# Two-layer transformer on one core: the last expert run writes its output tiles to their tokens' places, with new orders of work

## The reference

```
h = layernorm(x) * (1 + ca) + sa ;  x = x + ga * attention(h)
h = layernorm(x) * (1 + cb) + sb ;  x = x + gb * experts(h)
```

```
for e in range(16):
    h = silu(xf @ W1[e] + b1[e]) * (xf @ W11[e] + b11[e])
    y = y + (h @ W2[e] + b2[e]) * gates[:, e, None]      # gates: 0 for all but the best two
z = silu(xf @ Ws1 + bs1) * (xf @ Ws11 + bs11) @ Ws2 + bs2
```

## Time and profile before

| | us |
|---|---|
| median of three runs | 1138.53 (1136.83 to 1141.62) |
| the profiled execution's own time | 1138.8 |
| its span, first to last instruction | 1137.1 |
| PE busy | 893.5 (79%) |
| DVE busy | 803.9 (71%) |
| ACT busy | 550.6 (48%) |
| POOL busy | 436.4 (38%) |
| mean granted clock of TensorE | 0.887 |

### The profile page before, as it was taken

The page is one execution under the profiler, slowest core; times in us unless marked ns, Lnnn a source line. Parts: engine busy times, 40 slices in busy tenths (PEclk is TensorE's granted clock), DMA queues, the critical chain, the costliest instruction groups (busy, mean ns, idle before and its releaser), DMA issues.

```text
span 1137.1 us, 17345 instructions
## 1 busy us (share of the span) xinstructions
PE 893.5 (79%) x5709; PEld 560.6 (49%) x5709; DVE 803.9 (71%) x1942; ACT 550.6 (48%) x1353; POOL 436.4 (38%) x623
## 2 busy tenths in 40 slices
PE   7743076896798799779878898987989998997892
PEld 5422033454345447555333554444656665665692
DVE  4688988958998843357667766668667778846664
ACT  3635244345344324316544454534667755685372
POOL 0213253462393413203345224444542427834422
PEclk9866597898798899989988898879999988999797
DMA  7500000000100000232222102214347625362473
GB/s 215 173 0 1 1 0 1 1 0 1 32 1 1 1 1 1 85 102 91 68 74 94 66 1 65 85 46 160 124 126 228 193 76 161 107 202 69 146 239 108
DMA packets 69416, 89.49 MB, mean 79 GB/s; under 512 B 7072, under 2 KB 41520, under 8 KB 69296
## 3 DMA queue, kind: packets, MB, share of 16 engines
q1 hardware_dynamic: 67280, 84.20, 23.8%
q0 software_dynamic: 2048, 4.20, 1.2%
HBM read 62.56 MB, written 26.35 MB: 78 GB/s over the span
## 4 chain that ended last, share of the span: by engine, by line
PE 33%; DVE 11%; ACT 6%; issue 4%; POOL 3%; DMA 2%; SPq 0%; POOLq 0%; ACTq 0%; DVEq 0%
PE banks L870 8%; PE banks L1030 6%; DVE MX L1543 3%; PE banks L963 3%; PE banks L1004 3%; PE banks L901 2%; ACT PT L1861 2%; PE banks L970 2%; POOL oms L2046 2%; ACT yh L1795 1%; PE banks L912 1%; DVE sil L1493 1%; PE banks L1017 1%; PE banks L945 1%; ACT sil L1801 1%
## 5 line engine op out<-in xcount | busy, mean ns | idle before, releaser
L1543 DVE TENSOR_REDUCE MX<-banks 128x4 f32<-128x512 f32 (+2 forms) x192 | 199.2, 1043 | 74.1 <-PE banks L1004 73.2
L1861 ACT ACTIVATE PT<-banks 128x768 f32<-128x768 f32 (+1 forms) x192 | 167.6, 879 | 111.7 <-PE banks L963 111.1
L2023 POOL TENSOR_SCALAR_AFFINE_SELECT PT<-PT 128x256 f32<-128x256 f32 x256 | 107.2, 434 | 200.7 <-ACT PT L1861 200.4
L970 PE MATMUL banks<-KS,QS 32*128 32x512 f32 (+3 forms) x512 | 95.4, 418 | 22.5 <-DVE MX L1543 10.3
L1748 ACT ACTIVATE T<-Sb,GM 128x32 f32<-128x32 f32 x128 | 45.2, 353 | 123.4 <-DVE Sb L1419 123.3
L1030 PE MATMUL banks<-PT,VA 128*17 128x512 f32 (+3 forms) x1024 | 96.5, 475 | 9.8 <-DVE on L1566 8.8
L963 PE MATMUL banks<-QS,KS 32*128 32x128 f32 (+3 forms) x512 | 94.9, 412 | 7.9 <-ACT PT L1861 7.0
L870 PE MATMUL banks<-xgT,wg 128*128 128x128 f32 x616 | 84.3, 281 | 10.8 <-ACT ysb L1821 10.4
L936 PE MATMUL banks<-w,hid 128*128 128x128 f32 x448 | 69.9, 302 | 28.8 <-DVE hid L1489 19.9
L1493 DVE SCALAR_TENSOR_TENSOR sil<-sil,yh 128x256 f32<-128x256 f32 x109 | 47.4, 435 | 61.6 <-ACT sil L1801 61.2
L936 PEld LDWEIGHTS banks<-w,hid 128*128 128x128 f32 x448 | 62.7, 209 | 56.6 <-DVE hid L1489 35.5
(11 more groups left out here) (278 smaller groups left out, 1965.8 us busy)
## 6 DMA issues: line engine op xcount, KB each, us to landing
wg<-in_ffn_dram SPq DMA_DIRECT2D x77, 386.0 KB, 4.3
QS<-parts SPq DMA_DIRECT2D x16, 512.0 KB, 3.7
KS<-parts SPq DMA_DIRECT2D x16, 512.0 KB, 4.6
yb<-ysb SPq DMA_DIRECT2D x17, 256.0 KB, 3.9
parts<-HR SPq DMA_DIRECT2D x16, 256.0 KB
parts<-HR SPq DMA_DIRECT2D x32, 128.0 KB
parts<-LO SPq DMA_DIRECT2D x32, 128.0 KB
xg<-xs SPq DMA_DIRECT2D x16, 256.0 KB, 4.5
```

Source lines behind the costliest of these rows:

```text
L970: e.matmul(where[op][:, k, nk * step:nk * step + nk], QS[lo:lo + 32, t % SLOTS, 128 * qb:128 * qb + 128], KS[lo:lo + 32, t % SLOTS, 0:nk], ...
L1543: v_mx.at(e.tensor_reduce(MX[n % 2][:, u:u + nm, qb % 2, 2 * pair:2 * pair + 2, 24].rearrange("p s i -> p i s"), p4, AX.X, ALU.max, negate ...
L1861: a_p.at(e.activation(PT[q % 3][:, 2 * pair:2 * pair + 2, :], where["score", q, pair][:, :, 0:n], ACT.Exp, scale=ISQ8))
L2023: ins = e.affine_select(out=pt, in_=pt, compare_op=ALU.is_ge, fill=0.0, base=0, pattern=[[0, 2], [1, 128]], channel_multiplier=-1)
```

## The change

The last group (g = 2, batch 3) gets another way out; the groups before are as they were. A token row carries in a 129th number the row of the output buffer `yd` to which its result belongs: 1 + 128 i + p for k = 0, 512 more for k = 1; a row that no token fills carries a place of its own behind the first 1025, from `c_empty`, a new input that is copied into `xs[2]` in the beginning. `ids` reads these numbers from the loaded chunk (for the picked chunk 0 from an extra load `firsts`), `keep` writes all 23 tiles into SBUF buffers of their own, and `send(j)` scatters tile j on POOL by an indirect DMA. When all are there, four plain loads (`regain`) bring the rows to `yg`. The four sums of batch 3 come first on DVE, then its four `moe_x`. The offsets of both layers are set anew: in layer one 60 lines of the listed order of PE differ, 156 of DVE, 142 of ACT, 32 of POOL; in layer two 162 of PE, 212 of DVE, 149 of ACT, 183 of POOL, 100 of SP, those of the new jobs with them. Among the moves: on PE mod(1) goes ahead of norm(0, 0) at the start, and ab(1) leaves its place between two convolutions; on ACT tok(0, 1) goes ahead of turned(0, 2); on POOL `length` of group 3 goes ahead of one half step of the MoE sum and two products (`o_pw`), and on DVE `invlen` of group 3 comes one scan step later; in layer two the first `qk_in` goes ahead of `v_in` on PE and ACT and ahead of `up0` on DVE. POOL's order around the last group is: eight spreads, send(0), seven collects of batch 2, send(1), the eighth collect, sends 2 to 8, sends 9 to 12 among the four `moe_x` of batch 2, sends 13 to 22.

```diff
+            gate_t_1=-4.0, turn_2=-1.0, qk_in_0=-2.7, norm_6=-1.0, rms_t_2=-0.7, route_4=1.5, o_back_1=0.3,
...
+              rms=-3.0, collect=7.0, moe_x0=13.5, wob=15.0, rms_p_3=-2.5, rms_p_1=-3.0, moe_x_1=18.0,
...
+              score_1=0.2, spread_1=2.5, send_22=24.5, send_20=3.5, send_0=-8.5, send_18=3.0, collect_2=3.0,
...
+    if g == 2:
+        table.append((e + 56, ("twin", 0)))
...
+        if g == 2:
+            table.append((a + step * tiles[0] + (gap - 6 if c >= picked else 8.0), ("ids", c)))
...
+            if g == 2:
+                table.append((t + 9 + (6 if c < picked else 0), ("send", j)))
...
+        if g < 2:
+            table += [(b + 1.4 * i, ("collect", batch, i % 2, i // 2)) for i in range(8)]
+        else:
+            table += [(b + 3 + 0.2 * i, ("regain", i)) for i in range(4)]
...
-             dk=3.0, share=-6.0, gate=1.5, gate_s=2.5, lam=-4.0, scan=-0.2, vb_2=7.5, ab_t_3=2.0, kb_0=3.0,
...
+             dk=3.0, share=-5.5, gate=1.5, gate_s=2.5, lam=-4.0, scan=-0.2, vb_2=7.5, ab_t_3=-7.5, kb_0=3.0,
...
-              length_3=7.0, o_state_2=-1.5, stat_2=6.5, o_gq_1=-8.0, ktd_0=12.0, o_pw_2=2.5, o_dk_2=2.0,
...
+              o_state=-2.0, length=-4.5, o_gq=-9.0, moe_x_0=17.0, o_gq_2=-10.5, o_ol_1=4.5, length_3=-7.5,
...
+        wide = sb("xm1", [128, 4, 129])
+        own = VAb[0][:, :, :, :].rearrange("p a h d -> p (a h d)")
+        twins, firsts = (own[:, 516 * i:516 * i + 516].rearrange("p (i d) -> p i d", i=4) for i in range(2))
+        lasts = [PT[1 + j // 12][:, :, :].rearrange("p a (t d) -> p (a t) d", d=128)[:, j % 12, :] for j in range(RUN[2])]
+        xm = [sb("xm0", [128, 4, 128])[:, :, :], wide[:, :, 0:128]]
...
-        xs, yb = ([nc.dram_tensor(f"{name}{g}", (RUN[g] * 128, 128), F32).ap() for g in range(3)] for name in ("xs", "yb"))
+        xs = [nc.dram_tensor(f"xs{g}", (RUN[g] * 128, (128, 128, 129)[g]), F32).ap() for g in range(3)]
+        yb = [nc.dram_tensor(f"yb{g}", (RUN[g] * 128, 128), F32).ap() for g in range(2)]
+        yd = nc.dram_tensor("yd", (1 + 1024 + 128 * RUN[2], 128), F32).ap()
...
+            if n == 3:
+                return (d_ys[0], d_ys[1], d_xg[0], d_xg[1])[i], (128, 128, 160, 176)[i]
...
+            def ids(c):
+                m, cc = len(CHUNKS[2][c]), CHUNK0[2] + c
+                if c < PICKED:
+                    v.wait_ge(d_zero, 64)
+                    here = firsts[:, 0:m, 128]
+                else:
+                    v.wait_ge(d_xg[cc % 2], 16 * (cc // 2 + (0 if c % 2 == 0 else 1)))
+                    here = xg[cc % 2][:, 0:m, 128]
+                v_ids.at(e.tensor_copy(yid[:, 4 * c:4 * c + m], here))
...
+                if h == 1:
+                    a.wait_ge(d_cd, 32)
+                    e.activation(wide[:, :, 128], cd[:, 1064:1068], ACT.Copy)
...
+            def twin(_):
+                a.wait_ge(v_xm, 8)
+                a.wait_ge(p_pv, 72)
+                e.activation(twins[:, :, 128], cd[:, 1068:1072], ACT.Copy)
+                a_tb.at(e.activation(twins[:, :, 0:128], xm[1], ACT.Copy))
...
+                if g == 2:
+                    a.wait_ge(p_pv, 96)
+                else:
+                    a.wait_ge(d_ys[cc % 2], 16 * (cc // 2))
+                a_ys1.at(e.activation(lasts[j] if g == 2 else ysb[cc % 2][:, j % 4, :], where["unit", u][:, 0:128], ACT.Copy, scale=0.5))
...
-                e.indirect_dma_start(xs[g], bass.IndirectOffsetOnAxis(posi[n][:, k, i:i + 1], 0), xm[n % 2][:, i, :],
+                rows = xm[n % 2][:, i, :]
+                if n == 3:
+                    rows = (wide, twins)[k][:, i, :]
+                    if k:
+                        g_.wait_ge(a_tb, 7)
+                e.indirect_dma_start(xs[g], bass.IndirectOffsetOnAxis(posi[n][:, k, i:i + 1], 0), rows,
+                                     None).then_inc(d_spread.sem, 16)
+
+            def send(j):
+                c = j // 4
+                g_.wait_ge(a_ys1, TILE0[2] + j + 1)
+                g_.wait_ge(v_ids, 4 + c + 1)
+                e.indirect_dma_start(yd, bass.IndirectOffsetOnAxis(yid[:, j:j + 1], 0), lasts[j],
...
-            for g in range(3):
+            for g in range(2):
                 load(xs[g].rearrange("(c p) d -> p c d", p=128), None, d_zero,
                      zt[:, :].unsqueeze(1).broadcast_to([128, RUN[g], 128]))
+            load(xs[2], "c_empty", d_zero)
...
+                if g == 2 and c > PICKED + 1:
+                    sp.wait_ge(v_ids, 4 + c - 1)
+                load(xg[cc % 2][:, 0:m, :] if g == 2 else xg[cc % 2][:, 0:m, 0:128], None, d_xg[cc % 2],
                      xs[g][512 * c:512 * c + 128 * m, :].rearrange("(c p) d -> p c d", p=128))
+                if g == 2 and c == PICKED + 1:
+                    sp.wait_ge(p_pv, 72)
+                    load(firsts, None, d_zero, xs[g][0:512, :].rearrange("(c p) d -> p c d", p=128))
...
-                if j == CHUNKS[g][c][-1]:
+                if g < 2 and j == CHUNKS[g][c][-1]:
...
+            def regain(i):
+                sp.wait_ge(d_spread, 512 + 16 * RUN[2])
+                sp.wait_ge(v_sum, 12)
+                load(yg[:, i:8:4, :], None, gathered(3, i)[0], yd[1:1025, :].rearrange("(k i p) d -> i p k d", k=2, i=4)[i])
...
+                                  (1 + 128 * np.arange(8) + np.arange(128)[:, None]).astype(np.float32)], 1)
+    empty = np.zeros((128 * RUN[2], 129), np.float32)
+    empty[:, 128] = 1025 + np.arange(128 * RUN[2])
+    o["c_empty"] = empty
```

More of the change, by code:

```diff
@@ L109 @@
 LATE = dict(
[L110 to L118, removed]
@@ L119 @@
-    ACT=dict(up0=3.0, down0=2.5, score=1.3, qk_in=1.0, v_in=1.0, norm=5.0, turn_x=3.0, up=2.0, rms_t=1.5,
[L120 to L125, removed]
@@ new lines @@
+    DVE=dict(up0=1.5, top=1.1, top_t=6.3, qk_in=1.5, up=2.7, down=6.7, route=0.1, place=-2.5, w_o=0.5, rms=-2.7,
+             rms_o=1.5, sum=5.2, norm=-2.0, pick=-8.0, moe_x=-1.5, stat=-4.5, o_norm=-3.3, blend=2.5,
+             place_2=0.5, sum_1=7.0, norm_7=-4.5, route_7=-3.5, place_3=-6.0, rms_3=1.5, stat_4=2.0, route_5=0.5,
+             pick_0=1.5, down_2=-6.0, moe_x_3=26.5, sum_3=4.0, up_11=-0.5, w_o_1=-0.5, blend_3=-9.0, rms_o_1=0.5,
+             ids_3=4.0, up_10=0.5, route_6=-1.0, down_0=-8.8, rms_o_3=1.0, rms_0=3.4, w_o_2=-1.0, qk_in_0=-3.0,
+             rms_o_2=0.5, top_t_2=1.0, o_norm_0=3.0, rms_1=1.0, up_12=-1.7, route_4=1.5, qk_in_3=-0.5, up0_4=0.5),
@@ L130, in front_table @@
+    SP=dict(moe_x=20.0, keep=-11.0, fetch=-15.0, bring=-5.5, fetch_1=5.5, moe_x_0=6.0, bring_2=-12.0,
+            keep_2=-4.5, fetch_2=-3.5, bring_1=7.5, divide=-2.5, gather=-4.5, regain_0=-10.0, keep_0=-8.0,
+            bring_0=-5.5, fetch_0=-2.0, gather_3=-2.5))
 def front_table(b):
@@ L230 @@
 LATE0 = dict(
[L231 to L234, removed]
-            ab_t_2=-8.0, o_turn_1=1.0, norm_3=1.3, ab_t_3=-6.5, vq_t_2=-6.5, down_3=1.5, o_out_3=1.5, up0_4=-2.5,
-            norm_0=-1.5, o_tok_3=1.0, up_1=-2.0, down_0=0.5),
@@ L245 @@
-    ACT=dict(qkv=12.5, conv=3.0, turned=2.5, k_t=5.0, vq_t=20.0, ab_t=9.0, o_sum=4.0, o_tok=8.5, o_turn=8.3,
-             route=11.5, up=0.5, up0=9.0, down0=20.0, tok=-2.2, scan=1.2, mod=-15.0, decay=-1.0, norm=2.5,
-             diag=-4.0, route_0=5.0, lam_0=1.0, conv_1=1.0, norm_3=1.0, diag_2=7.0, norm_0=6.5, k_t_2=3.0,
-             tok_3=-5.0, tok_1=2.5, tok_0=3.0, norm_1=7.5, route_2=-2.0, tok_2=6.0, diag_1=5.0, decay_0=-4.5,
-             turned_1=1.0, down_3=2.0, scan_0=1.0, up_3=1.0, down=0.3),
@@ new lines @@
+    ACT=dict(qkv=13.7, conv=3.0, turned=2.5, k_t=5.0, vq_t=20.0, ab_t=9.9, o_sum=4.0, o_tok=8.5, o_turn=8.0,
+             route=10.5, up=0.5, up0=9.0, down0=20.0, tok=-2.9, scan=1.5, mod=-15.0, decay=-1.0, norm=2.5,
+             diag=-4.0, route_0=5.0, lam_0=1.0, conv_1=3.2, norm_3=1.0, diag_2=7.0, norm_0=6.5, k_t_2=3.0,
+             tok_3=-5.0, tok_1=-3.0, tok_0=3.0, norm_1=7.5, route_2=1.0, tok_2=4.5, diag_1=5.0, decay_0=-4.5,
+             turned_1=3.0, down_3=3.5, scan_0=0.3, up_3=3.0, down=0.5, vq_t_1=-8.0, up_1=0.5, ab_t_3=-8.0,
+             vq_t_3=-17.0, o_turn_2=-2.0, mod_1=-11.5, qkv_3=-1.5, o_tok_3=-1.5, conv_0=3.5, diag_0=-3.0,
+             o_sum_2=3.0, o_turn_1=-2.2, ab_t_1=-2.0, turned_0=4.0, o_turn_0=-1.0, scan_1=0.3, route_3=1.5,
+             o_sum_1=3.5, scan_3=-0.5),
@@ L1872, in rms_t @@
                 a_to.at(e.activation(oTs[k][:, :], where["rms_t", b, k][:, :], ACT.Copy))
-            jobs = dict(up0=up, down0=down, turn_x=norm, table=table, mod=mod, lam=lam_, tok=tok_, diag=diag, norm=norm, route=route, qkv=qkv, decay=decay, conv=conv,
+            jobs = dict(up0=up, down0=down, turn_x=norm, table=table, twin=twin, mod=mod, lam=lam_, tok=tok_, diag=diag, norm=norm, route=route, qkv=qkv, decay=decay, conv=conv,
                         turned=turned, k_t=k_t, vq_t=vq_t, ab_t=ab_t, scan=scan, o_sum=o_sum, o_tok=o_tok, o_turn=o_turn,
@@ L2195, in gather @@
                          parts[q % 2][256 * i:256 * i + 256, :].rearrange("(u p) t -> p u t", u=2))
```

(2 more changed lines are left out.)

67 lines of the change are left out of this document (44 added, 23 removed).

## The result

The changed kernel takes 1127.33 us (median of 8 runs, 1123.79 to 1133.13) against 1137.91 for the kernel before in the same comparison (8 runs, 1132.67 to 1142.21): ratio 0.9911, 95% interval 0.9888 to 0.9935, so about 10 us faster. The forecast was 1132.3, a fall of 6.5. The new kernel is faster: the interval leaves out 1.

A forecast was written before the change was run, and what follows sets the result against it. Limits differ by stage: VectorE in layer one's scan, PE in the last layer, then weight loads and DMA. From 1138.8 us, +1.5 − 4.5 − 2 − 2.5 + 0 + 1 = −6.5 gave 1132.3 us, range 1122 to 1142.

The forecast's parts named there:

- A: Start: mod(1)'s matmuls ahead of norm(0, 0) on PE delay the first qkv; +1.5 us, between 0 and +3.5.
- B: Layer one's scan: group 3's `length` earlier on POOL and `invlen` later shorten DVE's longest stop; −4.5 us, −8 to −1.
- C: Layer two's start: first query and key piece ahead of the values, round trip starts earlier; −2.5 us, −3 to 0.
- E1: Layer one's other moves: ACT's part of scan steps comes earlier, cutting DVE's waits for `T`; −2 us, −8 to +3.
- E2: Layer two's middle: reordered jobs, no wait above 1 us seen on the chain; 0 us, −5 to +4.
- D: Tail behind the last keep: scattering instead of gathering, with POOL's queue as the bound; +1 us, −4.7 to +8.
- Rival (1): Tail: POOL isn't the bound, so it ends 5.8 us sooner, total 1126.5 us; chance 0.15.
- Rival (2): New orders' gains are taken back, PE being as full as DVE; 1140.8 or 1139 us; 0.17 including an unshortened stop.
- Rival (3): Tail: small transfers slow it, POOL's indirect DMAs queueing behind `firsts`; +8 us there, total 1144.8; chance 0.12.

The follow-up runs named there:

- before_again: The kernel before, unchanged, traced again in the third comparison, where the kernel before took 1151.5 us.
- two_moves: Kernel before with only group 3's `length` ahead on POOL and layer two's first `qk_in` ahead on PE, ACT, DVE; ran once: scan 317.5 us, no ratio given.
- first_half_new: Kernel before with the new offsets of layer two only for jobs due before 425; ratio to the kernel before 0.9963.
- orders_only: Kernel before with all new offsets of both layers except the last run of tiles, no scattering; ratio to the kernel before 0.9921.
- second_half_new: Kernel before with layer two's new offsets only for jobs due from 425 on, without the last run's; ratio to the kernel before 0.9943.

## Why the prediction was right, and where its sizes were off

- **Direction and size.** Forecast −6.5, measured −10 (0.9911), and −7 beside the other kernels (0.9938). The mechanism named for the gain, the new orders and not the scattering, is what the runs show; the shares of its terms are not. That the sum came out near is in part luck: the terms ahead of the attention (A, B, C, E1) were put at −7.5 and brought under 3, and E2, put at 0, brought the rest.
- **D, the tail, +1:** 73.2 against 72.6 from `posi` on in the first pair, +0.6. POOL is the bound, by 7.0 instead of 5.8. `firsts` landed in 4.8 (1062.33 to 1067.1) instead of 4.1; the send in 2.24 instead of 2.8 and the plain load in 2.12 instead of 2.3; the sums and outputs took 4.8 instead of 5.7, since instructions of one kind follow each other without the gaps between sum and output. The Trainium skill, "DMA: Bandwidth & Descriptors", section "Anatomy of one DMA — SWDGE (gpsimd) path", which gave an estimated 2.15 for a send, was nearer to the trace's 2.24 than my 2.8. Rival (1), POOL not the bound, is what the later comparisons have; its −5.8 is there (9.7 instead of 15.6 behind the keep), and I had not seen that the run ahead of it can get longer by as much.
- **A, the start, +1.5:** 0. The first qkv starts at 18.98 instead of 18.55, +0.4 and not the 2.6 worked out, and the first scan step is unmoved (66.4 and 66.5). The modulation that was put ahead starts at 10.17 instead of 11.72, so it takes less of norm's time than its own length.
- **B, `length`, −4.5:** the step that failed. The words "this step (1.3 us) runs inside the stop" and "5.4 less idle" left out that the step ends with a wait for ACT's `T`, which comes no earlier than the sums of squares (5.25 of waiting in the changed kernel), and that `length` also overtook `OL` and `OTm` of POOL, which then, with the products behind them, hold DVE for 3.4 (1.95, 1.42 and 0.77 instead of 0.17, 0.29 and 0.29). What stays at this place is 1.1. B and E1 together, −6.5, measured −2.2 (means of 319.6 and 317.4 of the scan).
- **E1, −2:** its ground, ACT's part of the step coming earlier, isn't what the trace shows: the waits for `T` grew from 14.4 to 24.1 in total, of which 5.25 are at B's place. Where the rest of the scan's gain comes from stays open.
- **C, −2.5:** −1.4 alone, and about −0.5 within the whole change (means 103.6 and 103.1).
- **E2, 0:** the largest term. "I see none with a wait above 1 us on the chain" was no ground for nothing: in a stretch where PE is 87% busy, dozens of stops of 0.5 to 2 us are what is left to gain. From the first of the maxima to `posi` the means fell from 575 to 569 (six traces with the old orders of the second half, seven with the new). Behind `posi` comes a part that the sum had nowhere: 85.0, 85.5 and 84.6 up to DVE's end in before_again, two_moves and first_half_new, and 81.5 and 82.8 in orders_only and second_half_new, which gather too. The orders of the second half made most of both.
- Rival (2), the gains taken back, is B's case, but not the whole. Rival (3), the small transfers: if the longer run is theirs, their price is 3 to 6 us of the run, not the +8 of a queue on POOL, and the shorter way out covers it.

## What to carry to other kernels

Before a removed stop is priced, ask two things. Which later instruction of the same engine waits for the same event by another way? Here the step put inside the stop needed `T`, which ACT makes behind the same sums. And what does the neighbour's order look like once one job is pulled ahead? Everything that it overtakes now runs beside the instructions that the stop used to hold back. When an order of thousands of jobs is set anew, price the many short waits of the fullest engine as a sum (the waits view of the stretch), not one by one. And when a change shortens the way behind the last job, look at what its new transfers share with the loads that the last job waits for.
